# Fewer row fetches by SyncE and none by ScalarE in a three-round graph network kernel, with GpSimd paced by landed rows

## The chip, the cores and the metric

One core of a Trainium2 chip runs the program. The metric is the device time in microseconds (us), lower is better; three executions were timed. PE or TensorE is the matrix engine, DVE or VectorE the vector engine, ACT or ScalarE the activation engine, POOL or GpSimd the engine that issues the indirect gathers, SP or SyncE the engine that issues most plain DMAs.

## The reference

A graph of 12,500 nodes of 128 floats and 200,000 edges, sorted by destination. Each round gathers one 128-float row for each edge, weights it, and sums the rows by destination node. The first layer does this twice (with four relations), the second once, so every edge's row is gathered three times.

```python
h = jnp.maximum(_layernorm(x, axis=-1), 0.0)
# _L0_gnn_ref: two of these, relu between them; ew = edge_weight scaled to 0..1
xj = x[src]                                   # 200,000 rows of 512 bytes
for r in range(4):
    m = m + (edge_type == r)[:, None] * (xj @ W[r])
m = m * edge_weight[:, None]
out = segment_sum(m, dst, num_segments=12500) + x @ root + bias
# then
x = x + _L0_gnn_ref(h, ...)
h = jnp.maximum(_layernorm(x, axis=-1), 0.0)
x = x + (segment_sum(edge_weight[:, None] * h[src], dst) @ W.T + b)
```

## The kernel before, in words

The edges are cut into chunks of 128 (C = 1563 chunks, one edge on each of 128 partitions). Four chunks are a group (391 groups), four groups are a unit of 16 chunks (NU = 98 units, the last one of 11 chunks). There are three rounds, r = 0, 1, 2, and each goes over all 1563 chunks: round 0 gathers from table0 (the normalised x; its first four units, 64 chunks, come straight from x), round 1 from table1, round 2 from table2. A round can begin its gathers only when the table that it reads has been stored.

**Who fetches a chunk.** Nearly every chunk is fetched by one indirect gather of GpSimd (`gather`, L558): 128 rows of 512 bytes into one slot of the tile `rows`, which holds four units (RING). Chunk 12 of a unit (SK) can be fetched otherwise:

- By SyncE, in every fourth unit (SE = 4; `by_sp`), in round 0 from unit 7 on. SyncE loads OB = 8 byte addresses from the tile `single_at` into registers (L497) and then issues eight DMAs of one row each (L502) into the tile `spare`, which has two buffers. The 128 rows of a chunk are spread over four units of its program (`singles`): 32 rows in each, or, for the first such chunk of rounds 1 and 2, 64 rows in each of the first two. They lie in its queue between the stores of table1, table2 or the output and the loads of `x_rows` and `h_rows`.
- By ScalarE, in rounds 1 and 2, in every eighth unit (AE = 8; `by_act`, unit 9 to 89): the same, 16 rows in each unit, from the tile `act_at` into the tile `spare_a` (`act_rows`, L798).

With 71 chunks fetched by SyncE and 22 by ScalarE, GpSimd issues 4689 - 93 = 4596 gathers.

**What holds GpSimd.** Its queue is written out in order of chunks (`gather_unit`). Before a unit it waits for `s_idx`, the list of row numbers, which DVE writes when TensorE has used up the unit that held the same slots four units earlier. In addition, before the second chunk of every group (`paced`; in round 0 from unit SETTLED = 12 on) it waits for `s_begun`, which TensorE raises with the first matmul of each group: the group two before (LEAD = 2) must have been begun.

**What TensorE does.** For each chunk it waits until the rows have landed (`wait_rows`) and multiplies them with a window of weights by destination (L975 in round 0, L1016 in rounds 1 and 2), in order of chunks. DVE adds each group's sums into `acc` (L1223), ScalarE copies finished node tiles, TensorE multiplies them by the weights, and SyncE stores them.

Of the kernel before, what the change touches and what calls it, by code (L numbers as in the profile page):

```python
# [4 lines left out]
P = 128  # L5
CG = 4
UG = 4
# [6 lines left out]
EARLY = 6  # L14
OB = 8
SE = 4
AE = 8
LEAD = 2
# [5 lines left out]
def build(nc, x, src, dst, etype, weight, W1, root1, b1, W2, root2, b2, W3, b3, out):  # L24
# [16 lines left out]
    NO = NU // SE  # L41
    AO = NU // AE
    last_units = NU - (NI - 1) * RING
# [25 lines left out]
    with ctx:  # L69
        def sb(name, shape, dt=fp32):  # L70
            return ctx.enter_context(nc.sbuf_tensor(name, shape, dt))
# [18 lines left out]
        single_src, single_type = sb("single_src", [NO, P], i32), sb("single_type", [NO, P], i32)  # L90
        spare_a = sb("spare_a", [P, 2, D])
        act_src, act_type = sb("act_src", [AO, P], i32), sb("act_type", [AO, P], i32)
        act_at = [sb(f"act_at{r}", [AO, P], i32) for r in range(2)]
        single_at = [sb(f"single_at{r}", [NO, P], i32) for r in range(3)]
# [64 lines left out]
        s_agg, s_acc = sem("s_agg"), sem("s_acc")  # L159
        s_begun = sem("s_begun")  # L160
        s_single = [[sem(f"s_single{r}{b}") for b in range(2)] for r in range(3)]
        s_single_at = sem("s_single_at")
        s_single_list = sem("s_single_list")
        s_by_act = [sem(f"s_by_act{b}") for b in range(2)]
        s_idx_part, s_agg_part = sem("s_idx_part"), sem("s_agg_part")
# [71 lines left out]
        def is_single(r, u, k=SK):  # L237

            return k == SK and (by_sp(r, u) or by_act(r, u))

        def by_act(r, u):

            return r > 0 and u % AE == 1 and AE < u < AO * AE

        def act_number(r, u):

            return (r - 1) * (AO - 1) + u // AE - 1

# [13 lines left out]
        def wait_rows(eng, r, u, k):  # L262

            if u == NU - 1:
                eng.wait_ge(s_tail[k], 16 * (r + 1))
            elif is_single(r, u, k) and by_act(r, u):
                n = act_number(r, u)
                eng.wait_ge(s_by_act[n % 2], 16 * P * (n // 2 + 1))
            elif is_single(r, u, k):
                n = single_number(r, u // SE)  # L270
                so_far = len(range(n, single_number(r, 0 if r else 1) - 1, -2))
                eng.wait_ge(s_single[r][n % 2], 16 * P * so_far)
            elif k == SK:
                eng.wait_ge(rows_signal(u, k), single_gathers(r, u))
            elif k % CG < CG - 1:
                v = u % RING
                per_round = NI if v < last_units - 1 else NI - 1
                both = 2 if k % CG == CG - 2 else 1
                eng.wait_ge(s_row[v * UG + k // CG][k % CG], 16 * both * (r * per_round + u // RING + 1))

        def chunk_rows(r, u, k):

            if is_single(r, u, k) and by_act(r, u):
                return spare_a[:, act_number(r, u) % 2, :]
            if is_single(r, u, k):
                return single_buffer(single_number(r, u // SE))
            return rows[:, u % RING * UC + k, :]
# [65 lines left out]
        def _(eng):  # L353
# [54 lines left out]
            for to, arr in ((single_src, src), (single_type, etype)):  # L408
                eng.dma_start(to[:, :], arr[0:last].rearrange("(j c e) -> j c e", c=SE * UC, e=P)[:, (SE - 1) * UC + SK, :]
                              ).then_inc(s_single_list, 16)  # L410
            for to, arr in ((act_src, src), (act_type, etype)):
                eng.dma_start(to[:, :], arr[0:AO * AE * UC * P].rearrange("(j c e) -> j c e", c=AE * UC, e=P)[:, UC + SK, :]
                              ).then_inc(s_single_list, 16)

            for b in range(NB):
# [65 lines left out]
            def single_rows(r, j, lo, hi):  # L481

                n = single_number(r, j)
                if lo == 0:
                    if n == 0:
                        eng.wait_ge(s_single_at, 7)
                    elif n > 1:
                        r0, j0 = divmod(n - 1, NO)
                        u = j0 * SE + SE - 1
                        if r0 == 0:  # L490
                            eng.wait_ge(s_half, 2 * u + 2)
                        else:
                            eng.wait_ge(s_agg, (r0 - 1) * NU + u + 1)
                numbers, table = single_at[r], in_bytes[r]
                to = single_buffer(n).bitcast(mybir.dt.uint8)
                for p in range(lo, hi, OB):
                    found = nc.values_load_multi_w_load_instructions(  # L497
                        numbers[j:j + 1, p:p + OB], engines=(mybir.EngineType.SP,), min_val=0,
                        max_val=table.shape[1] - row_bytes,
                        skip_runtime_bounds_check_because="the lists name nodes of the graph alone")[1]  # L500
                    for k in range(OB):
                        eng.dma_start(to[p + k:p + k + 1, :], table[0:1, bass.ds(found[k], row_bytes)]  # L502
                                      ).then_inc(s_single[r][n % 2], 16)
# [43 lines left out]
        def _(eng):  # L547
# [14 lines left out]
            def gather_unit(table, r, i, v):  # L562
# [7 lines left out]
                for k in range(chunks_of(u)):  # L570
                    if halves and k == HC:
                        eng.wait_ge(s_idx, u + 1)
                    if paced(r, u, k):
                        eng.wait_ge(s_begun, u * UG + k // CG + (r * NG + 1 - LEAD))
                    if not is_single(r, u, k):
# [42 lines left out]
        def _(eng):  # L618
# [157 lines left out]

            def act_rows(r, u):

                j, part = divmod(u + AE - 1, AE)
                if not 0 < j < AO:  # L780
                    return
                n = act_number(r, j * AE + 1)
                if part == 0:
                    if j == 1:
                        eng.wait_ge(s_single_at, 7)
                        for s in range(2):
                            eng.wait_ge(s_stored[s], stored_by(r, s, 0))
                    if n > 1:
                        r0, j0 = divmod(n - 2, AO - 1)
                        eng.wait_ge(s_agg, r0 * NU + (j0 + 1) * AE + 2)  # L790
                table = in_bytes[r]
                for p in range(part * P // AE, (part + 1) * P // AE, OB):
                    found = nc.values_load_multi_w_load_instructions(
                        act_at[r - 1][j:j + 1, p:p + OB], engines=(mybir.EngineType.Activation,), min_val=0,
                        max_val=table.shape[1] - row_bytes,
                        skip_runtime_bounds_check_because="the lists name nodes of the graph alone")[1]
                    for k in range(OB):
                        eng.dma_start(spare_a[p + k:p + k + 1, n % 2, :].bitcast(mybir.dt.uint8),  # L798
                                      table[0:1, bass.ds(found[k], row_bytes)]).then_inc(s_by_act[n % 2], 16)

            def fast(r):

                def unit(i, v):
# [3 lines left out]
                    if not first(u, 1):  # L807
                        eng.wait_ge(s_acc, u * UG + (r * NG + UG) if not isinstance(u, int) else r * NG + min(u * UG + UG, NG))
                        prep(r, u - 1, (v - 1) % 2)
                    act_rows(r, u)  # L810
                units(unit)
# [37 lines left out]
        def _(eng):  # L849
# [99 lines left out]
            def first_round():  # L949
# [6 lines left out]
                def unit(i, v):  # L956
                    u = i * RING + v
                    for q in range(UG):
                        h = q // 2
                        if q in groups_of(u):  # L960
# [3 lines left out]
                            for k in range(n):  # L964
# [8 lines left out]
                                if k == CG - 1 and not raw and g < NG - 1:  # L973
                                    eng.wait_ge(s_wide, g + 2)
                                ins = eng.matmul(half_ps[v % 2 * 2 + h][:, q % 2 * RW:(q % 2 + 1) * RW], chunk_rows(0, u, q * CG + k),  # L975
                                                 wide[:, v % 2, q * CG + k, :], start=(k == 0), stop=(k == n - 1))
                                if k == 0:
                                    ins.then_inc(s_begun, 1)
                            if q % 2 == 1 or q == groups_of(u)[-1]:
# [19 lines left out]
            def fast(r):  # L999

                def unit(i, v):
# [5 lines left out]
                    for q in groups_of(u):  # L1007
# [3 lines left out]
                        for k in range(n):  # L1011
                            slot = v * UC + q * CG + k
                            wait_rows(eng, r, u, q * CG + k)
                            if k == CG - 1 and q == UG - 1 and RING - 1 <= u < NU - 1:
                                eng.wait_ge(s_window, u * 2 + ((r - 1) * 2 * NU + 4))
                            ins = eng.matmul(agg_of(u, v, q)[:, q * W:(q + 1) * W], chunk_rows(r, u, q * CG + k), window[:, slot, :],  # L1016
                                             start=(k == 0), stop=(k == n - 1))
                            if k == 0:
                                ins.then_inc(s_begun, 1)
                        if q == groups_of(u)[-1]:  # L1020
# [49 lines left out]
        def _(eng):  # L1070
# [117 lines left out]
            def clear_rest():  # L1188
# [3 lines left out]

            eng.wait_ge(s_single_list, 64)
            eng.tensor_scalar(single_at[0][:, :], single_src[:, :], float(row_bytes), None, ALU.mult).then_inc(s_single_at, 1)
            eng.tensor_scalar(single_at[2][:, :], single_src[:, :], float(2 * row_bytes), None, ALU.mult).then_inc(s_single_at, 1)
            eng.tensor_scalar(single_at[1][:, :], single_type[:, :], float(row_bytes), None, ALU.mult).then_inc(s_single_at, 1)
            eng.tensor_scalar(act_at[1][:, :], act_src[:, :], float(2 * row_bytes), None, ALU.mult).then_inc(s_single_at, 1)
            eng.tensor_scalar(act_at[0][:, :], act_type[:, :], float(row_bytes), None, ALU.mult).then_inc(s_single_at, 1)
            eng.wait_ge(s_single_at, 5)
            eng.scalar_tensor_tensor(out=act_at[0][:, :], in0=act_src[:, :], scalar=float(R * row_bytes),  # L1200
                                     in1=act_at[0][:, :], op0=ALU.mult, op1=ALU.add).then_inc(s_single_at, 1)
            eng.scalar_tensor_tensor(out=single_at[1][:, :], in0=single_src[:, :], scalar=float(R * row_bytes),
# [314 lines left out]
```

## Time and profile before

| what | value |
|---|---|
| device time, three executions | 7895.59 us median (7885.74 to 7914.38) |
| span of the profiled execution | 5774.9 us |
| own time of the profiled execution | not given by the page; only its span is |
| POOL busy | 4343.6 us, 75% of the span |
| PE busy | 3158.5 us, 55% |
| DVE busy | 1415.7 us, 25% |
| ACT busy | 439.1 us, 8% |
| rounds in the trace | round 0 to about 1942 us, round 1 to about 3859 us, round 2 to the end |

Two things have to be kept in mind when reading it. The span of the profiled execution is 2120.7 us below the median of the timed executions, and the page does not say where those lie. And the records of GpSimd's indirect DMAs cover its own work on the descriptors; the time until the rows have landed is listed apart. "Issue" before an instruction is time in which its engine waited for nothing that the profile shows.

### The profile page before, as it was taken

How to read it: one execution, taken by the hardware profiler on the slowest of the kernel's cores; microseconds unless marked ns; L12 is line 12 of the kernel's file. 1: busy time of each engine (PE TensorE's matmuls, PEld its weight loads, DVE VectorE, ACT ScalarE, POOL GpSimd, SP SyncE). 2: the span in 40 equal slices, each digit the busy share in tenths (PEclk: the TensorE clock that was granted, in tenths of full speed). 3: DMA queues.
4: the chain of work that ended last, by engine and by line, in shares of the span. 5: the costliest groups of instructions: out<-in, count | busy, mean ns of one | idle time of the engine just before them, and what ended most of it. 6: DMA issues, size and time to landing. Idle time of an engine off the chain costs nothing.

```text
span 5774.9 us, 61089 instructions
## 1 busy us (share of the span) xinstructions
PE 3158.5 (55%) x11399; PEld 2521.8 (44%) x11399; DVE 1415.7 (25%) x5042; ACT 439.1 (8%) x1183; POOL 4343.6 (75%) x4604
## 2 busy tenths in 40 slices
PE   3766666666666545444444444444444445444454
PEld 2655544544555434333334443434444444444443
DVE  7433333333333222122212222211111111111111
ACT  5111111111111000000000000000000000000000
POOL 7777777777777677777777777777777777777777
PEclk7878788788877655555555555555555555555555
DMA  6222222222222222222222222222222222222222
GB/s 173 82 76 74 73 75 74 73 75 74 73 75 74 61 62 62 61 60 62 62 60 61 62 62 60 62 59 60 62 62 60 62 62 60 62 62 61 60 62 58
DMA packets 285830, 392.59 MB, mean 68 GB/s; under 512 B 92011, under 2 KB 199360, under 8 KB 285440
## 3 DMA queue, kind: packets, MB, share of 16 engines
q0 software_dynamic: 147072, 301.50, 20.0%
q1 hardware_dynamic: 132736, 85.70, 4.9%
q14 instruction: 299, 2.45, 0.1%
q8 instruction: 91, 1.49, 0.1%
q10 hardware_dynamic: 5632, 1.45, 0.1%
HBM read 336.95 MB, written 51.34 MB: 67 GB/s over the span
## 4 chain that ended last, share of the span: by engine, by line
POOL 74%; issue 24%; PE 1%; DMA 1%; DVE 0%; ACT 0%; POOLq 0%; DVEq 0%
POOL rows L558 74%; DMA rows<-table,idx 1%; PE bank L975 0%; PE bank L915 0%; PE bank L893 0%; PE bank L908 0%; PE bank L923 0%; DMA table<-st 0%; DMA table<-sums 0%; DMA st<-in_src_dram 0%; PE bank L924 0%; DVE win L1342 0%; PE bank L1016 0%; DVE acc L1223 0%; POOLq L69 0%
## 5 line engine op out<-in xcount | busy, mean ns | idle before, releaser
L558 POOL DMA_INDIRECT rows<-table,idx x4532 | 4276.9, 944 | 1402.1 <-issue 1378.0
L1016 PE MATMUL bank<-win,rows 128*128 128x48 f32 x6112 | 1816.9, 424 | 1938.7 <-DMA rows<-table,idx 1917.4
L1016 PEld LDWEIGHTS bank<-win,rows 128*128 128x128 f32 x6112 | 1474.6, 317 | 2281.5 <-DMA rows<-table,idx 2261.1
L975 PE MATMUL bank<-win,rows 128*128 128x192 f32 x3080 | 850.0, 404 | 634.9 <-DMA rows<-table,idx 490.2
L975 PEld LDWEIGHTS bank<-win,rows 128*128 128x128 f32 x3080 | 587.4, 226 | 846.9 <-DMA rows<-table,idx 670.2
L1223 DVE TENSOR_TENSOR acc<-acc,bank 128x48 f32 x1173 | 237.8, 203 | 1106.0 <-PE bank L893 956.6
L1342 DVE TENSOR_SCALAR win<-iota,key,sw_col 128x192 f32<-128x192 f32 x1563 | 501.5, 391 | 18.2 <-PE bank L908 16.2
L688 ACT ACTIVATE tile_T<-acc 128x128 f32<-128x128 f32 x196 | 60.4, 309 | 2852.5 <-DVE acc L1223 2852.5
L1285 DVE TENSOR_SCALAR idx<-src_col 128x16 int32<-128x16 int32 x98 | 18.5, 191 | 829.7 <-PE bank L1016 829.7
L893 PE MATMUL bank<-sums,W1s 128*128 128x192 f32 (+1 forms) x784 | 218.7, 445 | 0.4 <-ACT sums L736 0.4
L1372 DVE TENSOR_TENSOR bank<-bank,rel 128x384 f32<-128x384 f32 x392 | 218.6, 558 | 0.7 <-issue 0.2
L1292 DVE SCALAR_TENSOR_TENSOR idx<-src_col,type_col 128x16 int32<-128x16 int32 x98 | 18.5, 191 | 772.1 <-PE bank L1016 772.1
L893 PEld LDWEIGHTS bank<-sums,W1s 128*128 128x128 f32 x784 | 205.1, 280 | 0.9 <-ACT sums L736 0.9
L1273 DVE TENSOR_TENSOR st<-bank,x_rows 128x128 f32<-128x128 f32 x98 | 28.6, 292 | 709.3 <-PE bank L947 709.3
L1094 DVE BATCH_NORM_STATS2 stats<-bank 128x6 f32<-128x128 f32 x98 | 29.2, 299 | 677.9 <-PE bank L945 677.9
L915 PE MATMUL bank<-W2s,tile_T 128*128 128x512 f32 x194 | 147.9, 858 | 0.0
L1376 DVE TENSOR_TENSOR win<-bank,w_col 128x384 f32<-128x384 f32 x196 | 109.0, 556 | 6.8
L1376 DVE TENSOR_TENSOR win<-bank,sw_col 128x384 f32<-128x384 f32 x196 | 109.0, 556 | 6.8
L623 ACT ACTIVATE std<-mv,eps 128x1 f32<-128x1 f32 (+3 forms) x127 | 37.2, 293 | 822.3 <-DVE mv L1100 822.3
L701 ACT ACTIVATE acc<-bank,b2s 128x128 f32<-128x128 f32 x98 | 36.0, 367 | 740.8 <-PE bank L924 740.8
L736 ACT ACTIVATE sums<-bank 128x384 f32<-128x384 f32 x196 | 85.6, 495 | 5.6 <-PE bank L975 5.6
L678 ACT ACTIVATE hT<-bank 128x128 f32<-128x128 f32 x98 | 27.2, 277 | 756.6 <-PE bank L901 756.6
(123 smaller groups left out, 1235.4 us busy)
## 6 DMA issues: line engine op xcount, KB each, us to landing
spare<-table SPq DMA_DIRECT2D x9088, 0.5 KB
rows<-table,idx POOLq DMA_INDIRECT x4532, 2.5
spare_a<-table ACTq DMA_DIRECT2D x2816, 0.5 KB
table<-st SPq DMA_DIRECT2D x146, 256.0 KB, 2.4
x_rows<-table SPq DMA_DIRECT2D x49, 128.0 KB
x_rows<-in_x_dram SPq DMA_DIRECT2D x48, 128.0 KB
h_rows<-table SPq DMA_DIRECT2D x48, 128.0 KB, 2.3
out_dram<-st SPq DMA_DIRECT2D x48, 128.0 KB, 2.1
```

The costliest lines, as they stand in the source:

```text
L558: eng.indirect_dma_start(out=rows[:, slot, :], out_offset=None, in_=table[:, :], in_offset=bass.IndirectOffsetOnAxis(ap=idx[:, slot:slot + ...
L623: eng.activation(std[:, p, 0:n], mv[:, p, 0:n, 1], ACT.Sqrt, bias=eps[:, 0:1]).then_inc(s_std, 1)
L688: eng.activation(tile_T[:, s, :], columns(t), ACT.Copy).then_inc(s_prep, 1)
L736: eng.activation(sums[:, v % 2, 2 * h:2 * h + w, :].rearrange("p g w -> p (g w)"), half_ps[v % 2 * 2 + h][:, 0:w * RW], ACT.Copy).then_inc ...
L893: ins = eng.matmul(mix_ps[:, 0:w], W1s[:, k, :], rhs(k), start=(k == 0), stop=(k == R - 1))
L915: eng.matmul(wide_of(t)[:, :], inner_of(t, s), W2s[:, :, :].rearrange("p r d -> p (r d)"), start=True, stop=True).then_inc(s_fin, 1)
L975: ins = eng.matmul(half_ps[v % 2 * 2 + h][:, q % 2 * RW:(q % 2 + 1) * RW], chunk_rows(0, u, q * CG + k), wide[:, v % 2, q * CG + k, :], st ...
L1016: ins = eng.matmul(agg_of(u, v, q)[:, q * W:(q + 1) * W], chunk_rows(r, u, q * CG + k), window[:, slot, :], start=(k == 0), stop=(k == n - 1))
L1223: eng.tensor_tensor(a, a, sums_ps, ALU.add).then_inc(s_acc, 1)
L1342: ins = eng.tensor_scalar(wide[:, v % 2, q * CG + k, :], iota[:, 0:RW], key0[:, bass.ds(c, 1)], sw_col[:, bass.ds(c, 1)], ALU.is_equal, AL ...
L1372: eng.tensor_tensor(match_ps[:, 0:n, :], iota_ps.unsqueeze(1).to_broadcast([P, n, W]), rel[:, bass.ds(c + lo, n)].unsqueeze(2).to_broadcas ...
L1376: eng.tensor_tensor(slots, match_ps[:, 0:n, :], wt[:, bass.ds(c + lo, n)].unsqueeze(2).to_broadcast([P, n, W]), ALU.mult).then_inc(s_windo ...
```

## The change

SyncE fetches chunk 12 of every eighth unit instead of every fourth (SE = 8), ScalarE fetches none (all of `act_rows`, its tiles, its lists and its semaphores go, with three small DVE instructions that made its addresses), and SyncE loads 16 addresses at a time (OB = 16), 16 rows in each unit. The chunks that are given up, 12 in round 0 and 23 in each of rounds 1 and 2, are gathered by GpSimd as the others are. The semaphore `s_begun` goes. In its place, on the same instructions of GpSimd's queue, stands a wait for the landing of rows: the third and fourth chunk of the group two before must be in `rows`.

```diff
-OB = 8
-SE = 4
-AE = 8
+OB = 16
+SE = 8
 LEAD = 2
...
         def is_single(r, u, k=SK):
 
-            return k == SK and (by_sp(r, u) or by_act(r, u))
-
-        def by_act(r, u):
-
-            return r > 0 and u % AE == 1 and AE < u < AO * AE
...
-                        eng.wait_ge(s_single_at, 7)
+                        eng.wait_ge(s_single_at, 4)
...
                     if paced(r, u, k):
-                        eng.wait_ge(s_begun, u * UG + k // CG + (r * NG + 1 - LEAD))
+                        w, q = divmod(u * UG + k // CG - LEAD, UG)
+                        if w >= 0:
+                            wait_rows(eng, r, w, q * CG + CG - 2)
                     if not is_single(r, u, k):
                         gather(table, v * UC + k, rows_signal(u, k))
...
-            def act_rows(r, u):
-
-                j, part = divmod(u + AE - 1, AE)
...
-                    act_rows(r, u)
...
-                                if k == 0:
-                                    ins.then_inc(s_begun, 1)
...
-            eng.wait_ge(s_single_list, 64)
+            eng.wait_ge(s_single_list, 32)
...
-            eng.tensor_scalar(act_at[1][:, :], act_src[:, :], float(2 * row_bytes), None, ALU.mult).then_inc(s_single_at, 1)
-            eng.tensor_scalar(act_at[0][:, :], act_type[:, :], float(row_bytes), None, ALU.mult).then_inc(s_single_at, 1)
...
```

On GpSimd, units 11 and 12 of round 0: the list for unit 11, its gathers, then the first paced unit. Before:

```order
44 L558 DMA rows<-table,idx 128x128 [waits s_idx]
45 L558 DMA rows<-table,idx 128x128 x14
46 L558 DMA rows<-table,idx 128x128 [waits s_idx]
47 L558 DMA rows<-table,idx 128x128 [waits s_begun]
48 L558 DMA rows<-table,idx 128x128 x3
49 L558 DMA rows<-table,idx 128x128 [waits s_begun]
50 L558 DMA rows<-table,idx 128x128 x3
51 L558 DMA rows<-table,idx 128x128 [waits s_begun]
```

The same place now (`s_row14_2` is the semaphore of the third and fourth chunk of the 15th group of the ring of 16):

```order
44 L534 DMA rows<-table,idx 128x128 [waits s_idx]
45 L534 DMA rows<-table,idx 128x128 x15
46 L534 DMA rows<-table,idx 128x128 [waits s_idx]
47 L534 DMA rows<-table,idx 128x128 [waits s_row14_2]
48 L534 DMA rows<-table,idx 128x128 x3
49 L534 DMA rows<-table,idx 128x128 [waits s_row15_2]
50 L534 DMA rows<-table,idx 128x128 x3
51 L534 DMA rows<-table,idx 128x128 [waits s_row0_2]
```

Unit 11 has 16 gathers where it had 15, and every paced wait stands before the same instruction as it did, on another semaphore.

On SyncE, unit 3 of round 0 before: a store of table1, then the second quarter of a chunk's rows in four lots of eight.

```order
49 L428 DMA table<-st 128x512 [waits s_fin_a]
50 L497 TENSOR_LOAD single_at
51 L502 DMA spare<-table 1x512 x8
52 L497 TENSOR_LOAD single_at
53 L502 DMA spare<-table 1x512 x8
54 L497 TENSOR_LOAD single_at
55 L502 DMA spare<-table 1x512 x8
56 L497 TENSOR_LOAD single_at
57 L502 DMA spare<-table 1x512 x8
58 L388 DMA h_rows<-table 128x2x128 [waits s_hturn]
```

Now the first such rows come in unit 6, and there are 16 of them to a unit:

```order
45 L404 DMA table<-st 128x512 [waits s_fin_a]
46 L368 DMA x_rows<-in_x_dram 128x2x128 [waits s_own]
47 L473 TENSOR_LOAD single_at [waits s_single_at]
48 L478 DMA spare<-table 1x512 x16
49 L404 DMA table<-st 128x512 [waits s_fin_a]
50 L473 TENSOR_LOAD single_at
51 L478 DMA spare<-table 1x512 x16
52 L368 DMA h_rows<-table 128x2x128 [waits s_hturn]
```

Between two stores SyncE issues 16 single rows with one load of addresses, where it issued 32 with four.

On ScalarE, the start of round 1 before: copying a node tile, then the first sixteen rows of a chunk.

```order
594 L688 ACTIVATE tile_T<-acc 128x128 [waits s_acc]
595 L793 TENSOR_LOAD act_at [waits s_stored1,s_stored0,s_single_at]
596 L798 DMA spare_a<-table 1x512 x8
597 L793 TENSOR_LOAD act_at
598 L798 DMA spare_a<-table 1x512 x8
599 L623 ACTIVATE std<-mv,eps 128x1 [waits s_mv]
```

Of these only the two activations are left in the changed program.

## Rows read from the trace of the kernel before

**Rows 1.** Page, part 1 and part 4: engines, and the chain that ended last.
```profile
PE 3158.5 (55%) x11399; PEld 2521.8 (44%) x11399; DVE 1415.7 (25%) x5042; ACT 439.1 (8%) x1183; POOL 4343.6 (75%) x4604
...
POOL 74%; issue 24%; PE 1%; DMA 1%; DVE 0%; ACT 0%; POOLq 0%; DVEq 0%
```

**Rows 2.** Page, part 5: groups; then GpSimd's other gathers by form (busy, mean ns, idle).
```profile
L558 POOL DMA_INDIRECT rows<-table,idx x4532 | 4276.9, 944 | 1402.1 <-issue 1378.0
...
L558 POOL DMA_INDIRECT rows<-in_x_dram,idx x64 | 64.5, 1008 | 20.4 <-issue 19.2 <-DVE idx L1088 1.2
```

**Rows 3.** Waits of POOL up to 1950 us, then after it: total us, times, longest.
```profile
POOL rows L558 <- issue: 447.7, 1468, 0.3
POOL rows L558 <- DMA table<-sums: 12.0, 1, 12.0
POOL rows L558 <- PE bank L975: 3.7, 12, 0.3
...
POOL rows L558 <- issue: 930.3, 3050, 0.3
POOL rows L558 <- DMA table<-st: 8.5, 1, 8.5
```

**Rows 4.** L558 by windows: length, busy (gathers), PE clock, DMA share, GB/s.
```profile
110.00:230.00 120.00, 90.72 (x97) 0.92 0.27 76
400.00:1900.00 1500.00, 1133.70 (x1202) 0.81 0.27 74
2100.00:3800.00 1700.00, 1284.59 (x1362) 0.50 0.23 61
4000.00:5700.00 1700.00, 1284.59 (x1363) 0.50 0.23 61
```

**Rows 5.** Timeline at the end of the span: the last gather and last DMAs.
```profile
5765.93 0.94 POOL L558 DMA_INDIRECT rows<-table,idx  x1 [0.30 <-issue]
...
5771.36 1.50 SPq L477 DMA_DIRECT2D out_dram<-st  x2
```

**Rows 6.** Gathers' landing: whole run, then 400 to 1950, then 3850 to the end.
```profile
DMA to landing us min/median/max: 2.4/2.5/7.0
...
DMA to landing us min/median/max: 2.4/2.5/4.0
...
DMA to landing us min/median/max: 2.4/2.5/3.8
```

**Rows 7.** SyncE and ScalarE's single rows: ns min/median/max, first and last start.
```profile
L502 SPq DMA_DIRECT2D spare<-table x9088: 227/228/440, 97.6 to 5678.1; - x198
...
L798 ACTq DMA_DIRECT2D spare_a<-table x2816: 213/213/532, 1989.0 to 5608.8; - x188
```

**Rows 8.** SyncE's timeline, early and later in round 1.
```profile
1944.15 82.85 SPq L502 DMA_DIRECT2D spare<-table  x192
...
2447.44 0.42 SPq L445 DMA_DIRECT2D table<-st  x1
2449.09 27.07 SPq L502 DMA_DIRECT2D spare<-table  x64
2486.14 0.42 SPq L445 DMA_DIRECT2D table<-st  x1
```

**Rows 9.** Matmuls that read spare, from the start of round 1.
```profile
L1016 PE MATMUL bank<-win,spare x4: 413/413/413, 2020.7 to 2099.6; 128*128 128x48 f32 x4
```

**Rows 10.** TensorE's longest waits: total us, times, longest.
```profile
PE bank L1016 <- DMA rows<-table,idx: 1917.4, 1773, 7.9
...
PE bank L975 <- DMA rows<-table,idx: 490.2, 484, 2.9
```

**Rows 11.** All engines from 2100 to 3800 us: busy time (instructions) of each.
```profile
2100.00:3800.00 1700.00, 838.48 (x2873) 676.90 (x2873) 352.32 (x1305) 92.33 (x261) 1284.59 (x1362) 0.50 0.23 61
```

More of the change, by code:

```diff
@@ L41, in build @@
     NO = NU // SE
-    AO = NU // AE
     last_units = NU - (NI - 1) * RING
@@ L90, in build @@
         single_src, single_type = sb("single_src", [NO, P], i32), sb("single_type", [NO, P], i32)
-        spare_a = sb("spare_a", [P, 2, D])
-        act_src, act_type = sb("act_src", [AO, P], i32), sb("act_type", [AO, P], i32)
-        act_at = [sb(f"act_at{r}", [AO, P], i32) for r in range(2)]
         single_at = [sb(f"single_at{r}", [NO, P], i32) for r in range(3)]
@@ L159, in build @@
         s_agg, s_acc = sem("s_agg"), sem("s_acc")
-        s_begun = sem("s_begun")
         s_single = [[sem(f"s_single{r}{b}") for b in range(2)] for r in range(3)]
@@ L163, in build @@
         s_single_list = sem("s_single_list")
-        s_by_act = [sem(f"s_by_act{b}") for b in range(2)]
         s_idx_part, s_agg_part = sem("s_idx_part"), sem("s_agg_part")
@@ L237, in is_single @@
         def is_single(r, u, k=SK):
-            return k == SK and (by_sp(r, u) or by_act(r, u))
-        def by_act(r, u):
-            return r > 0 and u % AE == 1 and AE < u < AO * AE
-        def act_number(r, u):
-            return (r - 1) * (AO - 1) + u // AE - 1
+            return k == SK and by_sp(r, u)
         def single_number(r, j):
@@ L265, in wait_rows @@
                 eng.wait_ge(s_tail[k], 16 * (r + 1))
-            elif is_single(r, u, k) and by_act(r, u):
-                n = act_number(r, u)
-                eng.wait_ge(s_by_act[n % 2], 16 * P * (n // 2 + 1))
             elif is_single(r, u, k):
@@ L281, in chunk_rows @@
         def chunk_rows(r, u, k):
-            if is_single(r, u, k) and by_act(r, u):
-                return spare_a[:, act_number(r, u) % 2, :]
             if is_single(r, u, k):
@@ L410, in _ @@
                               ).then_inc(s_single_list, 16)
-            for to, arr in ((act_src, src), (act_type, etype)):
-                eng.dma_start(to[:, :], arr[0:AO * AE * UC * P].rearrange("(j c e) -> j c e", c=AE * UC, e=P)[:, UC + SK, :]
-                              ).then_inc(s_single_list, 16)
             for b in range(NB):
@@ L775, in first_round @@
                     own_out(t)
-            def act_rows(r, u):
-                j, part = divmod(u + AE - 1, AE)
[L780 to L799, printed above, removed]
             def fast(r):
@@ L1017, in unit @@
                                              start=(k == 0), stop=(k == n - 1))
-                            if k == 0:
-                                ins.then_inc(s_begun, 1)
                         if q == groups_of(u)[-1]:
@@ L1196, in _ @@
             eng.tensor_scalar(single_at[1][:, :], single_type[:, :], float(row_bytes), None, ALU.mult).then_inc(s_single_at, 1)
-            eng.tensor_scalar(act_at[1][:, :], act_src[:, :], float(2 * row_bytes), None, ALU.mult).then_inc(s_single_at, 1)
-            eng.tensor_scalar(act_at[0][:, :], act_type[:, :], float(row_bytes), None, ALU.mult).then_inc(s_single_at, 1)
-            eng.wait_ge(s_single_at, 5)
-            eng.scalar_tensor_tensor(out=act_at[0][:, :], in0=act_src[:, :], scalar=float(R * row_bytes),
-                                     in1=act_at[0][:, :], op0=ALU.mult, op1=ALU.add).then_inc(s_single_at, 1)
+            eng.wait_ge(s_single_at, 3)
             eng.scalar_tensor_tensor(out=single_at[1][:, :], in0=single_src[:, :], scalar=float(R * row_bytes),
```

## The prediction

> **What bounds the kernel now.** I read the shares of the engines and the chain that ended last first. POOL is the busiest engine, 4343.6 us, and the chain gives 74% of the span to it and 24% to "issue" [rows 1]. The list of groups says what both are: 4532 gathers of L558, 944 ns each, with 1402.1 us of idle time before them, of which 1378.0 is issue [rows 2]. The list of POOL's waits leaves little else: 12.0 us at the start of round 1, 8.5 at the start of round 2, and 3.7 us in twelve waits put down to TensorE, none over 0.3 us, which is as long as any issue gap [rows 3]. So GpSimd issues one gather after another and in effect never waits for data, for TensorE or for a free slot.
>
> The pace is the price of a gather: (4276.9 + 1402.1 - 12.0 - 8.5) / 4532 = 1.2485 us. It can be read again in windows: 1500 us / 1202 = 1.248 in round 0, where ScalarE fetches nothing; 1700 / 1362 and 1700 / 1363 = 1.248 and 1.247 in rounds 1 and 2, where it does; 120 / 97 = 1.24 in units without the paced wait, equal to the others within one gather at the edge of so short a window [rows 4]. The clock of TensorE (0.92 to 0.50) and the DMA share (0.27 to 0.23) leave it alone.
>
> The other engines follow. TensorE waits for landing rows 1917.4 us in L1016 and 490.2 us in L975 [rows 10]; in the middle of round 1 it is busy 838.48 of 1700 us, DVE 352.32, ACT 92.33 [rows 11]. The end hangs on the last gather, at 5765.93 of 5774.9 us [rows 5].
>
> **The account against which the sum is made.** The page gives only the span, 5774.9 us; the timed median is 7895.59, so 2120.7 us are not in the trace. I take them as lying around the span and unchanged. If instead they are the same work at a slower pace, every term grows by 7895.59 / 5774.9 = 1.367. I keep both. By the Trainium skill, Runtime: NRT & Kernel Launch, the section on the launch sequence, what surrounds a kernel costs about 15 us, so by that page almost all of the 2120.7 us would be inside the execution and the second reading holds; no row here shows which.
>
> **The change part by part.**
>
> *More gathers.* SyncE's chunks fall from 71 to 35 (11 + 12 + 12), ScalarE's from 22 to none: 9088 and 2816 single rows [rows 7] are 71 and 22 times 128, after it 4480 and 0. GpSimd issues 4689 - 35 = 4654 gathers in place of 4596: 58 more, 12 in round 0 and 23 in each other round. All 58 lie on the bounding queue, nothing beside them: 58 x 1.2485 = +72.4 us. Bounds from the rows: at 944 ns, if the issue gap went, 54.8; at the 1.32 us of the first 64 gathers ((64.5 + 19.2) / 64 [rows 2]), 76.9; at the slower pace of the second reading, 99.0.
>
> *The paced waits.* Before and after, each stands on the second chunk of a group, so there are as many (but for two at the start of each later round). Paced and unpaced stretches have one pace, so a wait that is already satisfied costs nothing, and I take 0 for the swap. Is the new one satisfied? It wants the third and fourth chunk of the group two before. From the start of that fourth gather to the start of the waiting one there are six gathers, 7.5 us, or five, 6.2 us, where the group between leaves chunk 12 to SyncE. Landing takes 2.5 us at the median and at most 4.0 and 3.8 in the windows that are paced; the 7.0 of the whole run is from the unpaced start [rows 6]. So it is always satisfied with 2.2 us or more to spare. If it were not, GpSimd would stop with the rest of its unit behind it, and TensorE would starve.
>
> *The s_begun signals.* TensorE loses an increment on one matmul in four; it has half its time free, which hides a gain or a loss.
>
> *SyncE.* It issued 64 rows in 27.07 us, loads included, in every 38.7 us from store to store, and 192 rows in 82.85 us at the start of a round [rows 8]. Now it issues 32 in the same 38.7 us, under 14 us of work at the old price, and the larger loads can only lower their number. A chunk's rows are done two units before TensorE wants them, as before. In rounds 1 and 2 the first chunk is wanted in unit 7 and not 3: before, its 128 rows were issued by about 1944.15 + 55 = 1999 us and its first matmul ran at 2020.7 [rows 8, 9], 21 us later; now 80 us are added. The stores of tables wait less behind single rows. At the round's end no single rows are left in either version, so the 12.0 and 8.5 us stay. 0 us.
>
> *ScalarE and DVE.* 2816 row DMAs go from ACT's queue and three tiny instructions from DVE's start. Both queues wait for TensorE most of the time; GpSimd hides it. 0 us. Fewer small DMAs could free the DMA engines for the gathers, but round 0 without ScalarE's rows and round 1 with them have one pace [rows 4], so 0, with a gain of at most 4 ns a gather (944 against a fastest of 940, which is 18 us in all) kept as the lower end.
>
> *Late next.* No stall goes, so nothing new becomes late: TensorE has the same chunks to multiply in a slightly longer time, so its share in the middle of a round, 0.49, falls.
>
> *Sum.* 5774.9 + 72.4 = 5847.3 us of span. On the median: 7895.59 + 72.4 = 7968.0 us, +0.92%; by the second reading 7994.6, +1.25%. I forecast 7968, as the nearer to the rows that show something; the case's own range is 7895.6 + 54.8 - 18 = 7932 to 7995 and, with the 0.2% by which the timed runs differ, 7925 to 8010.
>
> The Trainium skill, Perfetto Trace Analysis, under DMA optimizations, advises to balance DMAs over the engines that can issue them where descriptor generation is the bottleneck. The trace agrees that it is (944 ns busy and 0.30 us gap, no waits), and the change shifts work the other way. The skill's DMA: Bandwidth & Descriptors, in the section on why a DMA increments its semaphore by 16, has a DMA of one partition run on a single, lowest-numbered engine; by it 11904 single rows crowd one engine, on which every gather also depends, and thinning them would speed landing. Landing sits at 2.5 us with and without ScalarE's rows [rows 6], so I give that nothing in the sum.
>
> **The rivals.**
>
> *A: single rows are what makes the timed runs longer (faster).* In the timed executions something takes 2120.7 us that the trace lacks. Its place would be SyncE's queue: TensorE stops at chunk 12 of a fourth unit for a late row, and as GpSimd waits for the beginning of a group, it stops within two groups. Against it: in the trace no wait on `spare` or `spare_a` appears, and SyncE uses 27 of 38.7 us. For it: only 11 us of each 38.7 are free, so single rows 1.4 times as dear would bind, and the coupling through `s_begun` passes such a delay on. The change halves SyncE's work and cuts the coupling. If all of the 2120.7 us hang on the 11904 rows (0.178 us each), the 7424 that go save 1323 and 58 gathers cost 72: 6645 us. It decides the sign once a removed row carries more than 72.4 / 7424 = 9.8 ns, that is 116 of the 2120.7 us. Chance 0.12.
>
> *B: a small relief offsets the gathers (no change).* Between 33 and 112 us would have to come back, from landing, from SyncE's stores or from a part of rival A: 7 to 24 ns a gather, where the steady windows differ by about 1 ns. Around 7895. Chance 0.08.
>
> *C: the landing wait binds (slower still).* If landing in the timed runs exceeded 6.2 us, GpSimd would pause in every group by the excess. At 7.0, the longest seen, it is 0.8 us on the groups behind a SyncE chunk, 35 in all: 28 us. At the 9 gathers' distance (11.2 us) that the old wait allowed, up to 3.7 us in each of 1121 paced groups, +4150, about 12,100. Paced landings of 4.0 at most speak against it. Chance 0.05, mostly above 8045.
>
> **How the numbers follow.** Forecast 0.75, A 0.12, B 0.08, C 0.05. A difference of 0.5% (39 us) is what a measurement of this kernel can tell from no change. The forecast's case and C are slower by more than that, but for the low end of its range (0.02): slower 0.78, within 0.5% 0.10, faster 0.12. The range 7880 to 8040 takes in the forecast's own range and the upper half of B; most of A and C, some 0.17, stay outside.
>
> **What would show it.** POOL with 4654 gathers at 944 ns and 0.30 us of issue, a pace of 1.248 in each round, a span near 5847, the three round boundaries later by about 15, 44 and 72 us; no wait of POOL for a landed row; single rows of SyncE at 4480 and of ScalarE at none. It would be wrong if the pace in those windows moved by over 16 ns (72.4 / 4654), if POOL showed waits on `rows`, or if the timed median moved while the span rose by 72: then the 2120.7 us are not a constant.

## The result and the profile after

The changed kernel took 7037.78 us (7032.72 to 7041.09, four runs) against 7896.16 us for the kernel before (four runs): ratio 0.8911, interval 0.8893 to 0.8928. It is 858 us faster, where 72 us slower was forecast and 7880 to 8040 was the range.

The profiled execution took 7041.09 us with a span of 7039.3. So the span is the time but for 1.8 us, and the 2120.7 us that the prediction put around the span of before cannot lie there: the trace of 5774.9 us was of an execution that took some 5777 us.

The page of the changed kernel, parts 1, 4 and 5, answers to [rows 1, 2]. The 65% of "another core or an unknown queue" are mostly waits of DVE for a matmul whose record the trace does not match:

```profile
PE 2581.5 (37%) x11399; PEld 2454.6 (35%) x11399; DVE 1388.9 (20%) x5039; ACT 439.9 (6%) x1183; POOL 4406.4 (63%) x4662
...
another core or an unknown queue 65%; DVE 14%; PE 10%; issue 9%; ACT 1%; DVEq 1%; DMA 0%; ACTq 0%; SPq 0%
...
L534 POOL DMA_INDIRECT rows<-table,idx x4590 | 4342.8, 946 | 2592.9 <-issue 1360.0
```

4590 + 64 = 4654 gathers at 946 ns, as forecast, but the idle time before them is 2592.9 us and not 1419. POOL's waits (total us, times, longest) answer to [rows 3]:

```profile
POOL rows L534 <- issue: 1379.3, 4478, 2.7
POOL rows L534 <- DVE idx L1231: 467.3, 75, 12.5
POOL rows L534 <- DVE idx L1237: 315.2, 47, 13.1
POOL rows L534 <- DVE idx L1230: 294.5, 47, 13.2
```

GpSimd waits for the lists idx, which come when TensorE has used up a unit. It is four units ahead and no longer the bound. What TensorE waits for is called issue, 2579.0 us in 1279 small steps before the matmuls of L967, and no wait of TensorE on spare appears. Its rows from 3962 us show the step:

```profile
PE bank L967 <- issue: 2579.0, 1279, 3.3
...
3964.16 0.24 PE L967 MATMUL bank<-win,rows 128*128 128x48 f32 x1 [2.56 <-issue]
3966.96 0.24 PE L967 MATMUL bank<-win,rows 128*128 128x48 f32 x1 [2.56 <-issue]
3969.76 0.24 PE L967 MATMUL bank<-win,rows 128*128 128x48 f32 x1 [2.56 <-issue]
```

One matmul in 2.8 us, and SyncE's timeline there answers to [rows 8]:

```profile
3941.89 44.02 SPq L478 DMA_DIRECT2D spare<-table  x32
3986.02 0.42 SPq L421 DMA_DIRECT2D table<-st  x1
3988.19 43.64 SPq L478 DMA_DIRECT2D spare<-table  x32
```

A row costs 44.02 / 32 = 1.38 us where before had 0.42, and SyncE goes from store to rows to store without a pause. By form (ns min/median/max) the time sits on single instructions, among them the register move, which waits for no data and took 29 ns each time in the trace of before:

```profile
L478 SPq MOVE spare<-table x4480: 2/29/1425, 311.4 to 7010.0; - x195
L478 SPq DMA_DIRECT2D spare<-table x4480: 2/228/1408, 312.2 to 7010.0; - x195
```

So two questions were open: in which condition the pair was timed, and which part of the change acts there. The theories: R, the single rows (SyncE's or ScalarE's) are the cost; P, the pace on s_begun is the cost; and later A, SyncE's dear rows hold TensorE and through it GpSimd.

### The profile page after: what moved, and what is told of

Its sections match the earlier page's. It is cut to its first block, busy times and chain, and to the rows that moved or that the text cites. A ratio compares the mean times of both kernels' runs of the same rounds, so it can differ in the third digit from the quotient of the medians.

```text
span 7039.3 us, 45081 instructions
## 1 busy us (share of the span) xinstructions
PE 2581.5 (37%) x11399; PEld 2454.6 (35%) x11399; DVE 1388.9 (20%) x5039; ACT 439.9 (6%) x1183; POOL 4406.4 (63%) x4662
## 3 DMA queue, kind: packets, MB, share of 16 engines
q14 instruction: 176, 1.44, 0.1%
## 4 chain that ended last, share of the span: by engine, by line
another core or an unknown queue 65%; DVE 14%; PE 10%; issue 9%; ACT 1%; DVEq 1%; DMA 0%; ACTq 0%; SPq 0%
DVE win L1287 5%; PE bank L967 5%; DVE acc L1168 3%; PE bank L928 3%; DVE bank L1317 2%; PE bank L846 1%; DVE win L1321 1%; PE bank L900 1%; DVE stats L1043 1%; DVEq L1168 0%; ACT tile_T L666 0%; DVE acc L1175 0%; PE bank L868 0%; ACT acc L606 0%
## 5 line engine op out<-in xcount | busy, mean ns | idle before, releaser
L534 POOL DMA_INDIRECT rows<-table,idx x4590 | 4342.8, 946 | 2592.9 <-issue 1360.0
L967 PE MATMUL bank<-win,rows 128*128 128x48 f32 x6204 | 1396.5, 375 | 2628.0 <-issue 2579.0
L967 PEld LDWEIGHTS bank<-win,rows 128*128 128x128 f32 x6204 | 1450.8, 324 | 2553.7 <-issue 2509.2
L928 PE MATMUL bank<-win,rows 128*128 128x192 f32 x3104 | 713.5, 381 | 1121.3 <-DVE win L1287 735.4
L1231 DVE COPY idx<-src_col 128x16 int32<-128x16 int32 x90 | 15.7, 175 | 706.4 <-remote 652.7
L900 PE MATMUL bank<-W3T,tile_T 128*128 128x128 f32 x196 | 76.9, 497 | 177.0 <-ACT tile_T L666 137.9
L898 PE MATMUL bank<-ident,tile_T 128*128 128x128 f32 x98 | 46.0, 472 | 212.4 <-ACT tile_T L666 187.6
L900 PEld LDWEIGHTS bank<-W3T,tile_T 128*128 128x128 f32 x196 | 49.8, 315 | 204.3 <-ACT tile_T L666 158.8
L868 PE MATMUL bank<-W2s,tile_T 128*128 128x512 f32 x194 | 113.4, 670 | 0.6 <-ACT tile_T L664 0.6
```

The source lines that it names most:

```text
L534: eng.indirect_dma_start(out=rows[:, slot, :], out_offset=None, in_=table[:, :], in_offset=bass.IndirectOffsetOnAxis(ap=idx[:, slot:slot + ...
L868: eng.matmul(wide_of(t)[:, :], inner_of(t, s), W2s[:, :, :].rearrange("p r d -> p (r d)"), start=True, stop=True).then_inc(s_fin, 1)
L900: eng.matmul(fin_of(t, s)[:, 0:D], tile_T[:, s, :], W3T[:, :], start=True, stop=True).then_inc(s_fin, 1)
```

## The experiments

The kernels of each part below ran on one chip, with before beside them: chips 1, 12, 13, 2 and 5, in this order.

**Chip 1: the parts apart.** e0_before is before, unchanged:

> The kernel before, unchanged, run and profiled again. Theory S (a slow issue): in the changed kernel's trace SyncE and TensorE issue one instruction in 0.7 to 1.4 us in stretches that begin some 10 us after GpSimd begins a run of gathers; the timed runs of before have such stretches too and the trace of 5774.9 us is of a run that lacks them. Then this run's span is within 5 us of its time, near 7890, and GpSimd waits for the lists idx or for the begun groups. Theory O (outside): the span is near 5775 again and the time near 7895, with 2120 us around the span.

5778.33 us, ratio 0.9998 (0.9988 to 1.0009); the profiled execution took 5778.79 us with a span of 5777.0. Neither theory held as put: span and time agree, but both near 5777.

e1_pace is before with the new pace:

```diff
-                        eng.wait_ge(s_begun, u * UG + k // CG + (r * NG + 1 - LEAD))
+                        w, q = divmod(u * UG + k // CG - LEAD, UG)
+                        if w >= 0:
+                            wait_rows(eng, r, w, q * CG + CG - 2)
```

> The kernel before with the new pace alone: the wait on s_begun replaced by the wait for landed rows; SyncE's and ScalarE's rows as before. Theory P (pace): GpSimd was held to TensorE's begun groups, so the new pace alone gives most of the gain: about 7050 to 7300 us. Theory R (rows): the single rows on SyncE and ScalarE are what costs, so this stays within 1% of 7896.

5778.96, ratio 1.000 (0.999 to 1.001). e2_few is the changed kernel with the old pace (the reverse edit):

> The changed kernel with the old pace: SyncE in every eighth unit, ScalarE none, but the wait on s_begun as before. Theory P: near 7900 or above (58 more gathers). Theory R: near 7040 to 7100.

5849.96, ratio 1.0125 (1.0108 to 1.0142). e3_unpaced is the changed kernel without any paced wait:

```diff
-            return k % CG == 1 and (r > 0 or u >= SETTLED)
+            return False
```

> The changed kernel with no paced wait at all; GpSimd is held by the lists idx alone. Since in the changed kernel's trace no wait for landed rows appears in GpSimd's waits, theory P expects no difference from the changed kernel: 7040 within 0.5%. If the landed-row wait does bind unseen, or bursts of gathers are what slows the others, this is slower by 1% or more.

5850.26, ratio 1.0124 (1.0107 to 1.0140). On this chip the pace is worth nothing in any form, and the swap of rows for gathers costs 1.25%, the opposite of the recorded result.

**Chip 12: the changed kernel itself.** f1_after is unchanged; f2_pace and f3_few repeat e1_pace and e2_few:

> The changed kernel, unchanged, beside before in the same call. In the last call before ran at 5779 us, not at 7896, and the changed kernel with the old pace or with none at 5850. Theory C (two conditions of the chip): the ratio depends on the condition. If before is near 5779 here, this is near 5850 (+1.25%, 58 gathers of 1.2485 us); if before is near 7896, this is near 7038. Theory D (the change itself is faster): the ratio is near 0.89 whatever before takes.

> Before with the new pace alone, again. If before is near 5779: 5779. If before is near 7896: theory P (pace) 7050 to 7300, theory R (rows) within 1% of 7896.

> The changed kernel with the old pace, again. If before is near 5779: 5850. If before is near 7896: theory P 7900 or above, theory R 7040 to 7100.

5847.35 against 5776.22, ratio 1.0123 (1.0106 to 1.0140); 5776.67; 5848.71. Theory C of f1_after (two conditions) fits and D (a ratio of 0.89 everywhere) falls. The rows of f1_after that answer to [rows 1 to 3] (engines; group; waits):

```profile
PE 3177.3 (54%) x11399; PEld 2536.5 (43%) x11399; DVE 1415.4 (24%) x5039; ACT 439.3 (8%) x1183; POOL 4397.1 (75%) x4662
...
L534 POOL DMA_INDIRECT rows<-table,idx x4590 | 4331.8, 944 | 1419.8 <-issue 1398.2
...
POOL rows L534 <- issue: 1417.4, 4650, 0.3
POOL rows L534 <- DMA table<-sums: 12.4, 1, 12.4
POOL rows L534 <- DMA table<-st: 8.6, 1, 8.6
```

and its windows, against [rows 4]:

```profile
2100.00:3800.00 1700.00, 835.40 (x2834) 670.48 (x2833) 347.77 (x1290) 91.25 (x258) 1284.92 (x1362) 0.50 0.23 60
4000.00:5700.00 1700.00, 834.11 (x2919) 691.06 (x2918) 275.12 (x860) 26.58 (x86) 1284.84 (x1363) 0.50 0.23 60
```

The same 1362 and 1363 gathers in 1700 us: the predicted picture, with a span of 5846.3 (5847.3 forecast). SyncE issues a row for 11.59 / 32 = 0.36 us and then pauses until the next store:

```profile
2904.80 0.41 SPq L421 DMA_DIRECT2D table<-st  x1
2906.98 11.59 SPq L478 DMA_DIRECT2D spare<-table  x32
2943.50 0.41 SPq L421 DMA_DIRECT2D table<-st  x1
```

g1_none takes the last single rows away (`is_single` returns False, `singles` issues nothing), g2_pace repeats e1_pace:

> The changed kernel with no single rows at all: GpSimd gathers all 4689 chunks. Where before runs at 5779: 35 more gathers of 1.2485 us than the changed kernel, 5847 + 44 = 5891. Where before runs at 7896: theory R (rows, or the instructions that issue them, cost the time) expects less than the changed kernel's 7038, by the same slope as before (7424 rows gave 858 us, so 4480 rows give 518): near 6520. Theory P (pace) expects 7038 + 44 = 7082.

> Before with the new pace alone, a third time. If before is near 5779: 5779. If before is near 7896: theory P (pace) 7050 to 7300, theory R (rows) within 1% of 7896.

5891.01 (forecast 5891) against 5776.64, ratio 1.0198 (1.0181 to 1.0215); 5776.7. Over the three counts of gathers, 4596, 4654 and 4689, one more costs 71.1 / 58 = 1.23 and 43.7 / 35 = 1.25 us.

**Chip 13: TensorE made the bound.** In the recorded trace of the changed kernel TensorE was late, so perhaps the coupling through s_begun costs only then. h1_begun is before with, in all rounds, 20 extra matmuls ahead of each group (the edit in rounds 1 and 2 is shown), h2_landed the same on e1_pace:

```diff
+                            for _extra in range(EXTRA if k == 0 else 0):
+                                eng.matmul(agg_of(u, v, q)[:, 2 * RW:2 * RW + W], chunk_rows(r, u, q * CG + k), window[:, slot, :],
+                                           start=True, stop=True)
```

> Before with 20 extra small matmuls ahead of each group on TensorE (into unused columns, the results are not read), so that TensorE and not GpSimd is the bound, as it was in the recorded trace of the changed kernel. GpSimd keeps the old pace (s_begun). At 0.31 us for a matmul at the full clock, 24 matmuls make 7.5 us a group against 5.0 of gathers: 9000 to 10500 us; more if the clock stays low. This run is one half of a comparison with h2_landed.

> The same extra matmuls with the new pace (landed rows). Theory P (the coupling to TensorE costs time where TensorE is late): over 3% faster than h1_begun. Theory R: the same as h1_begun within 0.5%, because TensorE sets the pace in both and only the place where GpSimd waits moves, from s_begun to the list idx.

> Before with the new pace alone, for the condition in which before takes 7896 if this call meets it: theory P 7050 to 7300, theory R within 1% of 7896. If before is near 5779: 5779.

11039.74 and 11040.86 us, before 5777.02; h3_pace 5777.11. I had put the time too low (TensorE's granted clock was 0.90 from 400 to 1900 us but 0.50 from 3500 us on). Between the two there is no difference. GpSimd's waits only change their name, first h1_begun, then h2_landed:

```profile
POOL rows L559 <- PE bank L1023: 4302.6, 756, 6.8
POOL rows L559 <- PE bank L979: 951.1, 343, 77.4
...
POOL rows L558 <- DVE idx L1289: 2026.7, 92, 23.0
POOL rows L558 <- DVE idx L1296: 1996.4, 92, 22.7
```

**Chip 2: single rows made dear.** A row of 1.38 us in the recorded trace of the changed kernel suggested theory A. i1_before is before with one address to a load on SyncE (a load per row), i2_after and i3_pace the same on the changed kernel and on e1_pace:

```diff
-OB = 8
+OB = 1
```

> Before with one address per load on SyncE (OB = 1 for SyncE, 8 kept for ScalarE), to make each of its single rows dearer: a load of 8 takes 0.79 us and one of 16 1.27, so one of 1 some 0.38, and a row 0.32 + 0.38 = 0.70 to 0.77 us where it took 0.42. Theory A (late rows of SyncE hold TensorE, and through it GpSimd): 128 rows and four stores take some 99 us where four units of gathers take 78, so 71 x 99 + 110 = 7140 us, 6800 to 7500. Theory N (single rows are hidden, or GpSimd does not care): 5779.

> The changed kernel with one address per load (OB = 1). The same dear rows, but half as many: 16 in a unit take some 12 us of 20. Both theories: 5847 within 0.3%. With i1_before at 7140 the change would then be worth -18% where rows are dear, though it costs 1.25% where they are cheap.

> i1_before with the new pace alone (landed rows instead of s_begun). Theory A with the coupling through s_begun (as my rival A put it): over 3% faster than i1_before, since GpSimd may run ahead. Theory A without it (SyncE alone sets the pace, GpSimd only waits elsewhere): the same as i1_before within 0.5%.

i4_after16 is the changed kernel with a load of 16 addresses before each single row:

```diff
-                for p in range(lo, hi, OB):
+                for p in range(lo, hi, EACH):      # EACH = 1
+                    b = p // OB * OB
```

> The changed kernel with a load of 16 addresses before every single row, so that a row costs 0.32 + 1.25 = 1.57 us, near the 1.4 us of the recorded trace of the changed kernel. Theory A: 128 rows and eight stores take some 214 us against 159 of gathers; SyncE issues rows without a pause, each chunk's last row is issued shortly before TensorE wants it, GpSimd waits for the lists idx: 35 x 214 + 160 = 7650, 7200 to 7950. Theory N: 5847.

| kernel | us | us per row | ratio to before (5778.05) |
|---|---|---|---|
| i1_before | 8532.33 | 28.13 / 32 = 0.88 | 1.4767 (1.4724 to 1.4810) |
| i3_pace | 8489.74 | | 1.4693 (1.4651 to 1.4736) |
| i2_after | 5848.43 | | 1.0122 (1.0093 to 1.0151) |
| i4_after16 | 7617.48 | 38.36 / 25 = 1.53 | 1.3184 (1.3145 to 1.3222) |

In i1_before and i4_after16 theory A holds. At 0.88 us a row the kernel before loses 2754 us and the changed one (i2_after) nothing, 5848.43 / 8532.33 = 0.685; at 1.53 us a row the changed one is held too. The new pace gives 43 us of the 8532, 0.5%: GpSimd, free to run ahead, is not what was lacking. i1_before lies above my 7140 mostly because a load of one takes 0.50 us and not 0.38, so that a row cost 0.88 and not 0.77. The waits in i1_before (total us, times, longest), then in i4_after16:

```profile
PEld bank L1016 <- DMA spare<-table: 1934.8, 48, 46.2
PE bank L1016 <- DMA spare<-table: 1927.0, 48, 46.0
POOL rows L558 <- PE bank L1016: 1847.1, 71, 39.8
```

```profile
PEld bank L969 <- DMA spare<-table: 918.9, 22, 46.9
PE bank L969 <- DMA spare<-table: 915.4, 22, 46.8
```

Forty-eight times in i1_before, once for each chunk of SyncE in rounds 1 and 2, TensorE stops for a single row, and GpSimd stops behind it; in i4_after16 it stops for 22 of the 24.

**Chip 5: a chip on which before takes the recorded time.** Here before took 7932.22 us, and its span was in it: 7921.8 us in an execution of 7923.67. k1_ae4 is before with AE = 4, k2_noact before without ScalarE's rows (`by_act` returns False, `act_rows` issues nothing):

> Before with ScalarE's rows in every fourth unit (AE = 4) and SyncE's as they are: 46 chunks on ScalarE, 24 gathers fewer. Where rows are cheap and GpSimd is the bound: 5777 - 24 x 1.2485 = 5747 us, a version faster than both kernels. If ScalarE's rows come late (32 rows take some 12 us of its 20 us unit) or delay its own copies, 5777 or above.

> Before with ScalarE's rows taken away alone: 22 more gathers, 5777 + 27.5 = 5804.5 us where rows are cheap. If this call meets the condition in which before takes 7896: theory A, SyncE sets the pace there, expects no change above 2% from taking ScalarE's rows away; a theory in which every issued instruction costs expects some 2816 of the 7424 removed rows' share, 300 us less.

k1_ae4: 8131.42, ratio 1.025 (1.0226 to 1.0275). k2_noact: 7892.22, ratio 0.9942 (0.9922 to 0.9962). More rows on ScalarE (3072, with 24 gathers fewer) cost 199 us here, and TensorE stops for each of their 46 chunks; none at all save 40 us in spite of 22 more gathers, which may be hidden, as GpSimd is not the bound. So ScalarE's rows are at most a small part of the 858 us. The wait on them in k1_ae4:

```profile
PEld bank L1016 <- DMA spare_a<-table: 1005.2, 46, 23.6
```

The chain that ended last in k2_noact, and the group of gathers:

```profile
SPq 59%; issue 38%; another core or an unknown queue 1%; DVE 1%; ACT 1%; POOL 0%; PE 0%; DMA 0%; DVEq 0%; ACTq 0%
SPq L502 48%; SPq L497 9%; SPq L428 0%; SPq L388 0%; POOL rows L558 0%; SPq L451 0%; ACT acc L628 0%; SPq L445 0%; DVE stats L1095 0%; SPq L471 0%; ACT rows L628 0%; DVE win L1343 0%; DVE mv L1101 0%; PE bank L976 0%
...
L558 POOL DMA_INDIRECT rows<-table,idx x4554 | 4297.5, 944 | 3513.5 <-issue 1284.3
```

SyncE's single rows, their loads and the issue gaps are nearly the whole chain; a gather still takes 944 ns. TensorE's waits on spare, then SyncE's timeline:

```profile
PEld bank L1017 <- DMA spare<-table: 1309.5, 48, 33.5
POOL rows L558 <- PE bank L1017: 1192.1, 108, 26.9
```

```profile
4990.79 12.86 SPq L502 DMA_DIRECT2D spare<-table  x32
5003.75 0.42 SPq L445 DMA_DIRECT2D table<-st  x1
5005.53 63.22 SPq L502 DMA_DIRECT2D spare<-table  x64
```

32 rows in 12.86 us, 0.40 each, while GpSimd stood still (20.78 us up to 5005.59), and then 64 in 63.22, 0.99 each, once gathers flowed again. Sorted by the gathers issued in the 8 us before, the median distance of two rows is 0.32 us after three or fewer, 1.44 after six and 2.10 after seven in this trace. In the recorded trace of the changed kernel it is 0.32 after two or fewer and 2.10 after six or more. In those of before and of f1_after it is 0.32 us with six or seven gathers too.

So rows are dear in both traces. But they hold TensorE in only one of them. DVE writes the list of row numbers for the unit four further on as soon as TensorE has used up a unit, and that write dates TensorE. A chunk of SyncE in round 1, its last row and the write for it, first in k2_noact (last row issued at 5003.4 us), then in the recorded changed kernel (4031.6 us):

```profile
4999.98 3.67 SPq L502 DMA_DIRECT2D spare<-table  x9
5006.63 0.17 DVE L1293 SCALAR_TENSOR_TENSOR idx<-src_col,type_col 128x16 int32<-128x16 int32 x1 [26.95 <-PE bank L1017]
...
4029.97 1.86 SPq L478 DMA_DIRECT2D spare<-table  x5
4076.26 0.17 DVE L1237 SCALAR_TENSOR_TENSOR idx<-src_col,type_col 128x16 int32<-128x16 int32 x1
```

The write came 3.2 to 4.2 us after the last row for all chunks of k2_noact but the first, and 3.2 to 4.4 us after it in i1_before; in the recorded changed kernel it came 42 to 53 us after it, for every chunk. (TensorE's own records cannot date this there: their names run some 30 us ahead of the semaphore that TensorE raises.) What stands on TensorE's path there is its own slow issue. SyncE had no time to spare either, with no wait from 2750 to 4750 us and 3.8 us of waits from 5000 to 7000, but nothing waited for its rows.

## Why the prediction was wrong

- **The sum of gathers: right in size, but not where the pair was timed.** +58 gathers, 1.2485 us each, +72.4: measured +71.1 on chip 12 (5776.22 to 5847.35), and the span of 5846.3 to within 1 us of the 5847.3 forecast. The swap of waits at 0 and SyncE, ScalarE and DVE at 0 held there.
- **The step that failed is the account.** "I take them as lying around the span and unchanged." Nothing of the kind lies around a span: span and time are 2 us apart at 5777 us (e0_before) and at 7924 us (before on chip 5). So the timed and the traced execution were in two conditions, 1.37 apart. My second reading, every term at a slower pace, failed too: gathers keep their 944 to 947 ns, and it is the issue of SyncE, ScalarE and TensorE that slows. I named that SyncE's queue could be the place and gave it 0.12.
- **SyncE at 0.** This term fell with the account. The "under 14 us of work" in 38.7, and the 27.07 us of before, stand on 0.42 us a row. Where a row costs 0.88, 32 rows to a unit outlast a unit of gathers (28 against 20 us) and SyncE is the bound. In k2_noact a chunk of SyncE followed the last one after 100 to 102 us in round 0 and mostly 106 to 114 later, where four units of gathers take 79. So the rows that the change takes away are on the path there and not hidden.
- **TensorE's issue at nothing.** "TensorE has the same chunks to multiply" left out that its matmuls can be issued late. In the recorded changed kernel this is what stands on the path, eight units taking 181 to 187 us in most of rounds 1 and 2 where the gathers need 159. That is the likely reason for 7038 and not 5847; no run isolates it.
- **Rival A: right in mechanism and sign, half right in its parts.** In k2_noact the late row and its place were as put, and single rows 2.1 times as dear did bind in i1_before. The price was put at 0.178 us a row if all 2120.7 us hung on them; the recorded pair gives (858 + 72) / 7424 = 0.125 on average, and as TensorE takes over as the bound, this is no price of a row. The cut coupling brought nothing where TensorE was the bound (h1_begun, h2_landed) and 0.5% where rows were (i3_pace).
- **Rival C: wrong.** No wait for landed rows appears in GpSimd's waits in any trace, the recorded one included; on chip 1 the ratio without the wait (e3_unpaced, 1.0124) is that of the changed kernel on chip 12 (1.0123).
- **The page on the launch.** By the Trainium skill's launch sequence in Runtime: NRT & Kernel Launch almost none of the 2120.7 us could be around the kernel. The trace agrees (1.8 us between span and time), and I had that sentence and chose against it.
- **The page on balancing DMAs** over the issuing engines (Perfetto Trace Analysis) fits where before takes 5777 us, by 1.2%: fewer fetches on the helpers is slower. In the recorded pair the advice speaks the wrong way: the engines that it would load more, SyncE and ScalarE, are the ones whose issue was dear, while a gather stayed at 946 ns.

Shown: the price of a gather; that nothing lay around the span; that dear single rows alone can turn the sign; that SyncE's rows end the chain of k2_noact on chip 5, and that in the recorded changed kernel they are issued 42 us or more before TensorE is done with their unit. Not shown: that the recorded pair ran on chip 5 (its times and its trace are of that kind), or that this is a matter of the chip and not of the time, since besides the pair only this one set of runs met it; how much of the 858 us is due to the rows and how much to the pace, since neither the new pace nor the changed kernel was run there; and why SyncE, ScalarE and TensorE issue slowly while gathers flow. Late loading of instructions is a rival for the last: a packet of its two queues took about as long (medians 1.02 and 0.45 us in the recorded changed kernel, 1.13 and 0.39 in f1_after), which speaks against it without ruling it out. Of the kernels run, the changed one is the fastest in the recorded condition and before on the other chips. k1_ae4 was expected to beat both where rows are cheap, 5747 by the sum, but ran only where they are dear.

## What to carry to other kernels

When a span and the timed median differ by much more than the 2 us seen here, do not add the difference as a constant: the trace is of another condition, and every margin in it must be read as a ratio. SyncE's 27 of 38.7 us was a margin of 1.4, and it was the first to go. Handing work to a helper queue pays 1.25 us a chunk where the helper keeps up, and costs the helper's whole lateness where it doesn't. The changed kernel's margin of 2.8 (under 14 of 38.7 us) survived rows 2.1 times as dear (i2_after) but not rows of 1.53 us (i4_after16). And date the engine that waits before calling a slow queue the bound: the recorded changed kernel had rows of 1.38 us and nobody waiting for them.

## What the runs showed of the hardware

The same program took 5776 to 5779 us on four chips and 7932 on another, with gathers of 944 ns on both and TensorE's granted clock at 0.50 in round 2 on both. On the slow one (k1_ae4, k2_noact) and in the recorded trace of the changed kernel, register moves that take 29 ns elsewhere took up to 1.4 us, on SyncE and ScalarE alike. The slow ones come in a step: of SyncE's 1723 moves over 0.3 us in the recorded trace, 1639 took 0.65 to 0.75 us. TensorE's matmuls came one in 2.8 us in long stretches of that trace. This goes with the flow of gathers: in k2_noact none of 1843 moves of SyncE was over 0.3 us when at most one gather had been issued in the 8 us before, and 1191 of 2246 were after six or more. After a pause of GpSimd of over 4 us in the recorded trace, the first such slow move came 8 us after the gathers resumed (median). ScalarE's, in k1_ae4 (ns min/median/max):

```profile
L798 ACTq MOVE spare_a<-table x5888: 3/29/1424, 2620.9 to 8035.0; - x197
```
